# First layer of a four-layer convolution kernel: 8192-byte input runs, mirrored channels stored once, preparation over six groups, channel weights in ten pieces

## The chip, the cores and the metric

The kernel runs on one core of a Trainium2 chip. The time is the device time of one execution, in microseconds (us); given are the median of three executions and one more that was profiled. Engine names: PE is TensorE, PEld its weight loads, DVE VectorE, ACT ScalarE, POOL GpSimd, SP the queue of SyncE that issues DMAs.

## What is computed

The input `x` is float32 of shape (4, 16, 512, 512): four images of sixteen channels. Four layers follow each other, each `x + conv(gn(x))` or the like, `gn` a group norm over pairs of channels. The change is in the first only; layers 1 to 3 (a quantised 3x3 convolution, a 17-wide box filter, a convolution in Fourier space) read its result. The first layer is two denoise blocks, one behind the other:

```python
def _gn(v, G=8, eps=1e-5):
    ...
    return ((g - m) / jnp.sqrt(s + eps)).reshape(v.shape)
def _triplets(x):
    prev = jnp.where(idx == 0, 1, idx - 1)
    nxt = jnp.where(idx == T - 1, T - 2, idx + 1)
    return jnp.stack([x[:, prev], x, x[:, nxt]], axis=2)
def _denoise_block(x, w1, b1, w2, b2, w3, b3, a, b, c):
    ...
    o = a * _conv_reflect(xf, w1, b1, 1, 2) + b * _conv_reflect(xf, w2, b2, 2, 4) + c * _conv_reflect(xf, w3, b3, 4, 8)
    return jnp.tanh(o).reshape(B, T, H, W)
x = x + _L0_conv_ref(_gn(x), ...)
```

Each output channel is made of three neighbouring channels (at the ends of an image the missing neighbour is the mirrored one: channel 1 stands before channel 0, channel 14 behind channel 15) by 5x5 taps at dilations 1, 2 and 4 with reflected borders, and a tanh. The second block takes the first one's output; the residual is added behind it.

## The kernel before

`layer0` holds both blocks. A **unit** u is one half (256 rows) of one pair of channels of one image; there are 64 units a block, 16 an image, in the order image, pair p (0 to 7), half. A unit has four **groups** of 64 rows, so there are 512 groups; group n = 4u+g is 100 matmuls of 128x512 on PE (`products`, lines 688 to 728). In the trace block 0 runs from 79.93 us (its first matmul) to 1602.02, block 1 to 2989.65.

Between the passes the data lie in DRAM as float16 in two parts (a high and a low one, so that the pair carries nearly float32): `xs` holds the normalised input for block 0, `ys` block 0's output for block 1. Both have nine **pair-groups** an image: pair-group 0 holds channels 1 (mirrored) and 0, pair-group p channels 2p−1 and 2p, pair-group 8 channels 15 and 14 (mirrored). One row of one channel, high and low part with its reflected borders, is 2112 bytes.

A unit reads a **window** `win[half]` (named c_w in the trace): 128 partitions, two pair-groups interleaved by partition, 16 blocks of 16 rows with the rows above and below. For p = 0 both pair-groups must be loaded, for p ≥ 1 only pair-group p+1, since the other one is in the buffer already. `load(u, g)`, lines 903 to 925, loads a half-window (two groups) in three parts per pair-group, of 48, 8 and 8 partitions and 7 or 8 blocks, and at the image's border a fourth of 40 partitions; each row of a block is a run of 2112 bytes. It waits until PE has finished group 4(u−2)+g+1, six groups before the loaded rows are used (line 908).

The order of each engine's work is written out by hand, group by group:
- PE, `products(u, g)`: 60 matmuls straight from the window, then, where it is due, one of the two small matmuls `p0`, `p1_` of the preparation (lines 680 to 686, called at 710 to 714), 16 more from the window, 16 from `near` (c_n), 8 from `twice` (c). Behind group 14 and group 17 come two matmuls for the channel weights (lines 754 to 760).
- DVE, lines 656 to 676: copies for the next group (`near` and `twice`, L637 to L640), a preparation step, in group 15 `channel_weights` and in group 22 `scaled_weights`, then the low part of the output (`low`, L609) or, in block 1, the residual sum and extremes.
- ACT: one or two copies for the next group, the tanh out of PSUM, the high part.
- POOL: reflected borders; in block 1 tables for a later layer.
- SP, lines 979 to 1003: stores of prepared input, window loads, stores of the output (`store_y`, one DMA per channel and group, three for p = 0 and 7), in block 1 `store_x1`, `load_res` and `store_table`. `load_res(u)` waits at lines 930 and 931 for the use of the buffer and for the stores of x1 out of it.

**Preparation of an input pair i** (of 32) runs in four consecutive groups, one step a group: `v0` statistics of all rows (eight `bn_stats`, one `bn_aggr`), `v1` mean, `v2` reciprocal deviation and normalisation, `v3` the low part. `p0` and `p1_` sum over partitions on PE between `v0` and `v1`, and `v1` and `v2`, each in the group after the step. Pair i's first group is given by

```python
            return 64 * image + 4 + 7 * j + 2 * (i == 3) if i > 2 else -2
```

so seven groups lie between pairs. `load_x` (lines 888 to 894) reads a pair as eight DMAs of 256 KB, partitions of rows r, r+16, ...; `store_xs` writes its two channels to `xs`, and for the first and last pair of an image the mirrored channel a second time. The first three pairs are prepared before block 0 starts.

The change touches, besides, `first_group`, `steps` and `loads_x` (L359 to L365), `n_xs`, `stored`, `rows_in` (L380 to L395), which count what has been stored and loaded, and `views` (L412).

Of the kernel before, what the change touches and what calls it, by code (L numbers as in the profile page):

```python
# [9 lines left out]
ALU = mybir.AluOpType  # L10
# [271 lines left out]
def layer0(K):  # L282
# [9 lines left out]
    with ExitStack() as ctx:  # L292
# [47 lines left out]
        a_ld = [sem(f"a_ld{i}") for i in range(2)]  # L340
        a_sd, a_bn, a_p, a_rt, a_g, a_hi, a_lo, a_pad, w_sw = (sem("a_" + n) for n in ("sd", "bn", "p", "rt", "g", "hi", "lo", "pad", "sw"))
# [38 lines left out]
        def n_xs(i):  # L380

            return 16 * sum(2 + (r % 8 in (0, 7)) for r in range(i))
# [9 lines left out]
        def rows_in(e, u, g):  # L392

            n = sum(1 + (place(r)[2] == 0) for r in range(u % 2, u + 1, 2))
            e.wait_ge(c_ld[u % 2][g // 2], 16 * (3 + at_edge(u % 2, g)) * n)  # L395
# [16 lines left out]
        def views(i):  # L412

            xr = xin[i % 2][:, :, :].rearrange("p c (r w) -> p c r w", w=NW)
            if i == 1:
                return [(xr[:, c], yt[c][:, :, 0, PAD:PAD + NW], yt[c][:, :, 1, PAD:PAD + NW]) for c in range(2)]
            return [(xr, *(h[:, :, l, PAD:PAD + NW].rearrange("p (c r) w -> p c r w", c=2) for l in range(2)))]
# [14 lines left out]
        with nc.Block() as block:  # L432

            @block.vector
            def _(v):
                def v0(i):
                    v.wait_ge(a_ld[i % 2], 128 * (i // 2 + 1))
                    for j in range(8):
                        v.bn_stats(ast[:, j, :], xin[i % 2][:, j // 4, 512 * (j % 4):512 * (j % 4) + 512]).then_inc(a_bn, 1)
                    v.wait_ge(a_bn, 8 * (i + 1))  # L440
                    mark["m", i] = ch.step(v, v.bn_aggr(am[:, 0, :], ast[:, :, :].rearrange("p a b -> p (a b)")))
# [16 lines left out]
                def v3(i):  # L458
                    v.wait_ge(a_hi, i + 1)
                    for xr, hi, lo in views(i):  # L460
                        t = v.tensor_tensor(lo, xr, hi, ALU.subtract)
                    t.then_inc(a_lo, 1)
# [64 lines left out]
                def channel_weights():  # L527
                    v.wait_ge(w13_ld, 160)
                    v.wait_ge(w13_p, 1)
                    ch.step(v, v.tensor_copy(rp[:, :, :].rearrange("p j n -> p (j n)"), pq[:, 0:432]))  # L530
                    ch.step(v, v.memset(qf[:, :, :], 0.0))
                    rq = rp[:, 0, :].rearrange("p (o y x) -> p y x o", y=3, x=3)
                    for ro in range(8):
                        for ky in range(3):
                            ri = ro + ky - 1
                            if 0 <= ri < 8:
                                dst = qf[:, :, 16 * ro:16 * ro + 16]
                                ch.step(v, v.scalar_tensor_tensor(dst, rq[:, ky], pt[:, ri:ri + 1], dst, ALU.mult, ALU.add))
                    ch.step(v, v.tensor_copy(wq[:, 0], qf[:, :, :]))
                    ch.step(v, v.tensor_tensor(wq[:, 1], qf[:, :, :], wq[:, 0], ALU.subtract))  # L540
                    ch.step(v, v.memset(qf[:, :, :], 0.0))
                    for s_, to, ky in ((0, 0, 0), (1, 112, 2)):
                        q0, q2 = qf[:, 0, to:to + 16], qf[:, 1, to:to + 16]
                        ts(q0, rq[:, ky, 0], pt[:, 40 + s_:41 + s_])
                        ch.step(v, v.scalar_tensor_tensor(q0, rq[:, ky, 1], pt[:, 42 + s_:43 + s_], q0, ALU.mult, ALU.add))
                        ts(q2, rq[:, ky, 2], pt[:, 40 + s_:41 + s_])
                    ch.step(v, v.tensor_copy(K.whq[:, 0], qf[:, 0:2]))
                    ch.step(v, v.tensor_tensor(K.whq[:, 1], qf[:, 0:2], K.whq[:, 0], ALU.subtract))
                    ts(ur[:, 0], rr[:, 1], 1.0)
                    tt(ur[:, 1], rr[:, 0], rr[:, 2], ALU.add)  # L550
                    tt(ur[:, 2], rj[:, 0], rj[:, 2], ALU.subtract)
                    ts(ui[:, 0], rj[:, 1], 1.0)
                    tt(ui[:, 1], rj[:, 0], rj[:, 2], ALU.add)
                    tt(ui[:, 2], rr[:, 2], rr[:, 0], ALU.subtract)
                    for t in range(3):
                        six(ur[:, t], ui[:, t], [gm[:, t, 16 * f:16 * f + 16] for f in range(6)])
                    g3 = gm[:, 0:3, :].rearrange("p t n -> p (t n)")
                    tt(tfb[:, :], g3, g3, ALU.mult)
                    mark["g3"] = ch.step(v, v.tensor_reduce(c2b[:, 0:1], tfb[:, :], AX.X, ALU.add))

                def scaled_weights():
                    g3 = gm[:, 0:3, :].rearrange("p t n -> p (t n)")
                    v.wait_ge(w13_p, 2)
                    mark["sv"] = inverse(v, ch, w13_rt, 1, pq[:, 0:1], c2b, sv)
                    ts(g3, g3, sv[:, 0:1])
# [79 lines left out]
                v0(0), v1(0), v2(0)  # L645
                v0(1), v1(1)
                v3(0)
# [3 lines left out]
                v3(1)  # L651
                pieces()
                norms()
                v0(2), v1(2)
                copies(0)
                for u in range(2 * NU):
                    blk, b, p, half = place(u)
                    for g in range(4):
# [3 lines left out]
                        if i is not None:  # L662
                            (v0, v1, v2, v3)[s](i)
                        if (u, g) == (3, 2):
                            mark["v"] = ch.n
                        if (u, g) == (3, 3):
                            channel_weights()
                        if (u, g) == (5, 2):
                            scaled_weights()
# [9 lines left out]
            def _(p):  # L679
# [8 lines left out]
                def products(u, g):  # L688
# [17 lines left out]
                    rows4 = buf[:, 4 * g:4 * g + 4]  # L706
                    for di in (4, 0, 1, 7, 8):
# [41 lines left out]
                p1_(2)  # L749
                p.wait_ge(a_v, mark["wc"])  # L750
                for u in range(2 * NU):
                    for g in range(4):
                        products(u, g)
                        if (u, g) == (3, 2):
# [3 lines left out]
                        if (u, g) == (4, 1):  # L758
# [4 lines left out]
            def _(s):  # L763
                def hi(i):
                    s.wait_ge(a_g, i + 1)
                    if i > 1:
                        s.wait_ge(a_sd, n_xs(i))
# [1287 lines left out]
```

## Time and profile before

| what | value |
| --- | --- |
| time, median of 3 | 5130.97 us (5124.47 to 5133.29) |
| time of the profiled execution | 5131.47 us |
| its span in the trace | 5129.7 us |
| block 0, first matmul to block 1's first | 79.93 to 1602.02 us |
| block 1 | 1602.02 to 2989.65 us |
| PE busy, whole span | 4772.3 us (93%) |
| DVE, ACT, POOL busy | 4133.9 (81%), 4039.3 (79%), 1532.3 (30%) |
| DMA packets | 501930, 1161.93 MB, mean 227 GB/s |

The lines of a trace name the engine, the line of the kernel, the operation and the tiles (written <- read). A bracket tells how long the engine was idle before the instruction and what ended that. In a list of waits a line reads "engine, tile and line that waited <- what it waited for: us in total, times, longest". Tile names: c_w window, c_n `near`, c `twice`, c_p the PSUM of a group, a_x the input pair, a_st and a_mv its statistics, a_p the PSUM of the small matmuls, c_t and c_y output tiles, qf and rp weights.

### The profile page before, as it was taken

To read this page: it belongs to the slowest core of one execution; us is meant where nothing else is said; L and a number is where in the kernel's file an instruction comes from. 1 tells how busy PE (TensorE), PEld (TensorE's weight loads), DVE (VectorE), ACT (ScalarE), POOL (GpSimd) and SP (SyncE) were. 2 spreads that over 40 slices of the span, in tenths; PEclk is the share of its full clock that TensorE was granted. 3 is DMA by queue.
4 is the path that set the end of the run, shared out by engine and by line. 5 is a ranking of instruction groups with operands and counts; after the bars stand their busy time and mean duration, and the time that the engine had idled before them with its cause. 6 is when DMAs were issued, how large, how long until landed. Compare 5 with 4: busy or idle time off the path is not lost. (4 is left out here: it accounts for less than half of the span.)

```text
span 5129.7 us, 174298 instructions
## 1 busy us (share of the span) xinstructions
PE 4772.3 (93%) x74557; PEld 2805.2 (55%) x74557; DVE 4133.9 (81%) x7219; ACT 4039.3 (79%) x4023; POOL 1532.3 (30%) x1643
## 2 busy tenths in 40 slices
PE   4799999999999999999999979997776999999998
PEld 2344444445455795565566744434555566666665
DVE  5786786876867888888888868888999688888888
ACT  3576776776767888888888887876997799999897
POOL 0111111111113222222222100004776355555556
PEclk9899999999999999999999989998999999999999
DMA  8899899999978778788778769996886466666654
GB/s 220 224 246 261 249 266 255 248 259 252 247 211 236 221 217 240 230 221 248 220 229 243 216 235 324 323 325 236 308 309 247 114 150 153 150 153 150 153 150 119
DMA packets 501930, 1161.93 MB, mean 227 GB/s; under 512 B 59593, under 2 KB 60232, under 8 KB 468042
## 3 DMA queue, kind: packets, MB, share of 16 engines
q1 hardware_dynamic: 499000, 1148.40, 77.0%
q8 instruction: 592, 9.70, 0.8%
q10 hardware_dynamic: 2162, 2.39, 0.2%
q14 instruction: 176, 1.44, 0.1%
HBM read 678.71 MB, written 453.51 MB: 221 GB/s over the span
## 5 line engine op out<-in xcount | busy, mean ns | idle before, releaser
L702 PE MATMUL c_p<-c_w,wc 128*32 128x512 f16 x38912 | 2270.7, 380 | 53.5 <-DMA c_w<-xs 48.2
L702 PEld LDWEIGHTS c_p<-c_w,wc 128*32 128x32 f16 x38912 | 1239.7, 96 | 935.9 <-issue 42.7
L792 ACT ACTIVATE c<-c_w 64x2052 f16<-64x2052 f16 x512 | 984.7, 1923 | 87.3 <-DMA c_w<-xs 74.9
L778 ACT ACTIVATE c_t<-c_p,cbias,cscale 128x512 f32<-128x512 f32 x512 | 398.1, 777 | 541.2 <-PE c_p L702 538.6
L702 PE MATMUL c_p<-c_n,wc 128*32 128x512 f16 x8192 | 589.8, 381 | 20.4 <-DVE c_n L638 19.3
L1780 PE MATMUL f_P<-f_qh,f_wt 64*64 64x512 f16 x4608 | 545.7, 378 | 1.8 <-DVE f_t L1676 1.8
L1780 PE MATMUL f_P<-f_hl,f_wt 64*64 64x512 f16 x4608 | 545.3, 379 | 0.0
L884 POOL COPY c_y<-c_y 128x16 f16<-128x16 f16 x512 | 191.1, 401 | 1070.6 <-DVE c_y L609 1070.6
L794 ACT ACTIVATE c<-c_w 64x2052 f16<-64x2052 f16 x256 | 492.9, 1925 | 6.3
L1941 POOL TENSOR_TENSOR f_y<-f_y,f_x 128x512 f32<-128x512 f32 x256 | 330.8, 1292 | 449.4 <-DVE f_hl L1655 443.3
L1540 POOL TENSOR_TENSOR e_hl<-e_g,e_hl 128x2048 f16<-128x2048 f32 x63 | 257.2, 4083 | 608.4 <-ACT e_hl L1490 608.4
L637 DVE COPY c_n<-c_w 96x2112 f16<-96x2112 f16 x512 | 389.7, 761 | 58.7 <-DMA c_w<-xs 58.7
L1676 DVE SCALAR_TENSOR_TENSOR f_t<-f_P,f_kk,f_ci 128x256 f32<-128x256 f32 x1024 | 423.6, 476 | 13.5 <-PE f_P L1780 7.9
L609 DVE SCALAR_TENSOR_TENSOR c_y<-c_t,c_y 128x512 f16<-128x512 f32 x256 | 176.9, 691 | 272.8 <-ACT c_y L788 270.9
L1741 PE MATMUL f_qp<-f_hil,f_gT 128*128 128x260 f16 (+1 forms) x3120 | 392.0, 275 | 4.1 <-DVE f_qh L1660 4.1
L702 PEld LDWEIGHTS c_p<-c_n,wc 128*32 128x32 f16 x8192 | 276.4, 96 | 211.3 <-DVE c_n L637 20.2
L638 DVE COPY c_n<-c_w 32x2112 f16<-32x2112 f16 x512 | 368.5, 720 | 15.9
L1780 PEld LDWEIGHTS f_P<-f_hl,f_wt 64*64 64x64 f16 x4608 | 233.0, 106 | 255.0 <-issue 77.7
L702 PE MATMUL c_p<-c,wc 128*32 128x512 f16 x4096 | 366.7, 381 | 3.2 <-issue 3.2
L1169 PE MATMUL d_pp<-d_q,wq 128*128 128x512 f16 x1536 | 345.8, 381 | 17.4 <-DVE d_q L1066 17.4
L1915 ACT ACTIVATE f_y<-f_P,f_kk,sv 128x256 f32<-128x256 f32 x512 | 260.9, 560 | 128.0 <-PE f_P L1780 121.8
L1947 POOL TENSOR_TENSOR f_t<-f_t 128x512 f32<-128x512 f32 (+1 forms) x260 | 333.2, 1282 | 70.5 <-DVE f_hl L1655 70.5
(275 smaller groups left out, 7681.6 us busy)
## 6 DMA issues: line engine op xcount, KB each, us to landing
d_x<-x SPq DMA_DIRECT2D x128, 1024.0 KB, 7.8
x<-d_x SPq DMA_DIRECT2D x128, 1024.0 KB, 5.1
ys<-c_y SPq DMA_DIRECT2D x576, 132.0 KB, 6.7
xs<-a_hl SPq DMA_DIRECT2D x70, 1056.0 KB, 10.1
a_x<-in_x SPq DMA_DIRECT2D x256, 256.0 KB, 7.1
a_x<-in_x SPq DMA_DIRECT2D x128, 512.0 KB, 5.0
x<-a_x SPq DMA_DIRECT2D x512, 128.0 KB, 5.3
f_x<-x SPq DMA_DIRECT2D x256, 256.0 KB
```

The costliest lines, as they stand in the source:

```text
L637: v.tensor_copy(near[n % 2][0:96], w[0:96, :, 0:PW]).then_inc(c_nh, 1)
L638: v.tensor_copy(near[n % 2][96:128], w[64:96, :, PW:RW]).then_inc(c_nl, 1)
L702: t = p.matmul(pg[32 * j:32 * j + 32, :], weights[:, var], source[:, j, at:at + NW], start=start, stop=stop, tile_position=(0, 32 * j))
L778: s.activation(tt_[n % 3][:, :], pp[:, n % 4, :], ACT.Tanh, bias=cbias[:, blk:blk + 1], scale=cscale[:, blk:blk + 1]).then_inc(c_act, 1)
L792: s.activation(twice[n % 2][64:128, :, PAD - 2:PAD - 1 + NW], w[0:64, :, PW + PAD + 1:PW + PAD + 2 + NW], ACT.Copy).then_inc(c_2b, 1)
L794: s.activation(twice[n % 2][0:64, :, PAD - 2:PAD - 1 + NW], w[0:64, :, PW + PAD - 2:PW + PAD - 1 + NW], ACT.Copy).then_inc(c_2c, 1)
L1169: t = p.matmul(pp[:, 4 * (i % 2) + j, :], wq[:, wl, dx, :], qt[i % NQ][:, j, dx:dx + NW], start=(i < 2 and dx == 0 and wl == 0), stop=(i > ...
L1676: v.scalar_tensor_tensor(dst[0:n, z], src[:, 256 * z:256 * z + 256], k_[0:n, off + z:off + z + 1], cc_[0:n, j, z], op, ALU.mult).then_inc( ...
L1741: t = p.matmul(qp[0:n, a_, 0:260], T[:, xl, 1 - a_, kx, 0:n], hil[:, wl, 1 - a_, kx, :], start=z == 0, stop=z == 5)
L1780: t = p.matmul(P[64 * z:64 * z + 64, bank, :].rearrange("p (a i) -> p a i", a=2), w[k0:k0 + 64, wl, f, :], r[k0:k0 + 64, l, :, 0:256], sta ...
L1941: q.tensor_tensor(y0[i % 3][:, :, :], y0[i % 3][:, :, :], par(xin[i % NXF][:, :]), ALU.add).then_inc(f_ax, 1)
L1947: q.tensor_tensor(t1[i % 3][0:n], t1[i % 3][0:n], t2[i % 2][0:n], ALU.add).then_inc(f_aw, 1)
```

## The change

- Input rows lie four consecutive ones to a partition: a channel is one DMA of 1 MB in runs of 8192 bytes, a pair two DMAs instead of eight.
- The mirrored channels are not stored any more: two stores a pair into `xs`, two a group into `ys`. Instead the window of the first and last pair of an image takes the mirrored channel from where it is stored anyway: for p = 0 pair-group 0, for p = 7 pair-group 8 are loaded as two half sources of every second partition (24, 4 and 4 partitions in place of 48, 8 and 8; `sources`).
- The preparation takes six groups: `v0` per channel, `v1`, `v2`, `v3` per channel; high part, mirror and store go by channel as well. `p0` stands in the group of step 2 (after 60 matmuls), `p1_` in that of step 3 (after 24). Pairs start two groups earlier.
- `channel_weights` is cut into ten pieces at groups 15, 18, 22, 25, 29, 32, 36, 39, 43 and 46, `scaled_weights` into two at 50 and 57; PE's matmuls for them follow groups 14 and 48.
- The stores and loads at the start are put in another order, and the first two units' loads wait for the three stores that they need alone.

```diff
-            return 64 * image + 4 + 7 * j + 2 * (i == 3) if i > 2 else -2
-
-        steps = {first_group(i) + z: (i, z) for i in range(2, NG) for z in range(4) if first_group(i) + z >= 0}
-        loads_x = {first_group(i - 2) + 4 + 2 * c: (i, c) for i in range(4, NG) for c in range(2)}
+            return 64 * image + 2 + 7 * j + (i == 3) if i > 2 else -3
+
+        steps = {first_group(i) + z: (i, z) for i in range(2, NG) for z in range(6) if first_group(i) + z >= 0}
+        parts_at = [15 + 7 * (z // 2) + 3 * (z % 2) for z in range(10)]
+        loads_x = {first_group(i - 2) + 6 + 2 * c: (i, c) for i in range(4, NG) for c in range(2)}
...
-            e.wait_ge(c_yd[u % 2], 16 * sum(8 + 4 * (place(r)[2] in (0, 7)) for r in range(u % 2, u, 2)))
+            e.wait_ge(c_yd[u % 2], 128 * (u // 2))
+
+        def sources(p):
+
+            outer = {0: [(0, (0,), 1, 0), (0, (1,), 0, 1)], 7: [(8, (0,), 8, 0), (8, (1,), 7, 1)]}
+            return outer.get(p, []) + [(p + 1, (0, 1), p + 1, 0)] * (p < 7)
...
+                def v0(i, c):
+                    v.wait_ge(a_ld[i % 2], 32 * (i // 2 + 1))
+                    for j in range(4):
+                        v.bn_stats(ast[:, 4 * c + j, :], xin[i % 2][:, c, 512 * j:512 * j + 512]).then_inc(a_bn, 1)
+                    if c:
+                        v.wait_ge(a_bn, 8 * (i + 1))
+                        mark["m", i] = ch.step(v, v.bn_aggr(am[:, 0, :], ast[:, :, :].rearrange("p a b -> p (a b)")))
...
+                    if part < 4:
+                        for ro in (2 * part, 2 * part + 1):
+                            for ky in range(3):
+                                ri = ro + ky - 1
+                                if 0 <= ri < 8:
+                                    dst = qf[:, :, 16 * ro:16 * ro + 16]
+                                    ch.step(v, v.scalar_tensor_tensor(dst, rq[:, ky], pt[:, ri:ri + 1], dst, ALU.mult, ALU.add))
...
                     for di in (4, 0, 1, 7, 8):
+                        if s == 3 and di == 1:
+                            p1_(i)
                         for wl, xl in ((0, 0), (0, 1), (1, 0)):
...
-                    i, s = stage_of(n - 1)
-                    if s == 0:
+                    if s == 2:
                         p0(i)
-                    if s == 1:
-                        p1_(i)
...
-                        e.wait_ge(a_lo, i - 1)
-                    for c, r in ((c, r) for c in channels for r in range(4)):
-                        e.dma_start(xin[i % 2][:, c, NW * r:NW * r + NW],
-                                    dram(x, ((b * NC + 2 * g + c) * NH + 16 * r) * NW, [[NW, 16], [64 * NW, 8], [1, NW]])).then_inc(a_ld[i % 2], 16)
+                        e.wait_ge(a_lo, 2 * (i - 1))
+                    for c in channels:
+                        e.dma_start(xin[i % 2][:, c, :], dram(x, (b * NC + 2 * g + c) * NH * NW, [[4 * NW, 128], [1, 4 * NW]])).then_inc(a_ld[i % 2], 16)
...
-                    for gp in (0, 1) if p == 0 else (p + 1,):
+                    for gp, slots, of, slot in sources(p):
                         for to, count, row, j, banks in parts:
-                            e.dma_start(win[half][to + gp % 2:to + 2 * count:2, 4 * g + j:4 * g + j + banks],
-                                        dram(src, pair(b, gp, 256 * half + 64 * g + 16 * j + row), [[RW, count], [16 * YP, banks], [1, RW]])).then_inc(c_ld[half][g // 2], 16)
+                            at = dram(src, pair(b, of, 256 * half + 64 * g + 16 * j + row, slot), [[(3 - len(slots)) * RW, count * len(slots) // 2], [16 * YP, banks], [1, RW]])
+                            first_p = to + gp % 2 + 2 * slots[0]
+                            e.dma_start(win[half][first_p:to + 2 * count:6 - 2 * len(slots), 4 * g + j:4 * g + j + banks], at).then_inc(c_ld[half][g // 2], 16)
...
-                    for m, gp, slot in [(0, p, 1), (1, p + 1, 0)] + [(1, 0, 0)] * (p == 0) + [(0, 8, 1)] * (p == 7):
+                    for m, gp, slot in ((0, p, 1), (1, p + 1, 0)):
...
-                store_xs(0)
+                store_xs(0, 0)
+                store_xs(0, 1)
+                store_xs(1, 0)
                 load_x(2)
-                store_xs(1)
+                store_xs(1, 1)
```

## Rows read from the trace of the kernel before

**Rows 1.** By stretch: length, busy PE, PEld, DVE, ACT, POOL, PEclk, DMA share, GB/s.

```profile
79.93:1602.02 1522.09, 1435.36 (x25720) 738.44 (x25724) 1137.64 (x1809) 1047.86 (x890) 250.05 (x594) 0.98 0.91 246
1602.02:2989.65 1387.63, 1385.82 (x25604) 886.42 (x25596) 1163.50 (x2042) 1181.30 (x768) 285.71 (x362) 1.00 0.78 226
```

**Rows 2.** Waits of PE, whole span: total us, times, longest us.

```profile
PE a_p L682 <- DVE a_mv L441: 63.3, 28, 19.0
PE c_p L702 <- DMA c_w<-xs: 48.2, 10, 15.0
PE c_p L702 <- DVE c_n L638: 19.3, 2, 13.9
```

**Rows 3.** Waits of PE, from 0 to 85 us.

```profile
PE a_p L682 <- DVE a_mv L441: 39.1, 3, 19.0
```

**Rows 4.** Waits of PE in block 1, 1602 to 2990 us.

```profile
PE c_p L702 <- issue: 1.8, 5, 0.4
```

**Rows 5.** Timeline of PE, 390 to 410: start, length, instruction, count.

```profile
394.70 3.42 PE L702 MATMUL c_p<-c_w,wc 128*32 128x512 f16 x60
...
401.49 3.41 PE L702 MATMUL c_p<-c_w,wc 128*32 128x512 f16 x60
...
407.32 2.98 PE L702 MATMUL c_p<-c_w,wc 128*32 128x512 f16 x52
```

**Rows 6.** Timeline of DVE, 392 to 400.

```profile
393.71 4.83 DVE L439 BATCH_NORM_STATS2 a_st<-a_x 128x6 f32<-128x512 f32 x8
398.57 0.37 DVE L441 BATCH_NORM_AGGREGATE a_mv<-a_st 128x2 f32<-128x48 f32 x1
398.98 0.69 DVE L609 SCALAR_TENSOR_TENSOR c_y<-c_t,c_y 128x512 f16<-128x512 f32 x1
```

**Rows 7.** Timeline of DVE, 199 to 210: the channel weights' longest run.

```profile
200.32 7.39 DVE L538 SCALAR_TENSOR_TENSOR qf<-rp,pt,qf 128x48 f32<-128x48 f32 x22
```

**Rows 8.** Timeline of PE around the weights; in brackets the wait before.

```profile
201.30 1.04 PE L702 MATMUL c_p<-c_n,wc 128*32 128x512 f16 x16
...
220.74 1.90 PE L702 MATMUL c_p<-c_n,wc 128*32 128x512 f16 x16 [13.86 <-DVE c_n L638]
...
267.29 1.90 PE L702 MATMUL c_p<-c_n,wc 128*32 128x512 f16 x16 [5.43 <-DVE c_n L638]
...
269.81 5.10 PE L702 MATMUL c_p<-c_w,wc 128*32 128x512 f16 x76
```

**Rows 9.** Timeline of PE at the start: first, fourth and fifth half-window.

```profile
79.93 6.13 PE L702 MATMUL c_p<-c_w,wc 128*32 128x512 f16 x76 [12.94 <-DMA c_w<-xs]
...
118.53 5.62 PE L702 MATMUL c_p<-c_w,wc 128*32 128x512 f16 x76 [3.07 <-DMA c_w<-xs]
...
147.70 5.52 PE L702 MATMUL c_p<-c_w,wc 128*32 128x512 f16 x60 [15.03 <-DMA c_w<-xs]
```

**Rows 10.** By stretch: first window loads, one image edge of block 1.

```profile
64.40:118.50 54.10, 35.95 (x604) 19.14 (x604) 24.83 (x38) 23.46 (x19) 3.93 (x12) 0.99 0.94 198
1917.00:1990.00 73.00, 72.29 (x1334) 43.90 (x1330) 59.15 (x103) 61.60 (x41) 12.76 (x17) 1.00 0.87 244
```

**Rows 11.** PE timeline, image edges of block 0: first and last of six.

```profile
505.08 4.29 PE L702 MATMUL c_p<-c_w,wc 128*32 128x512 f16 x76 [3.48 <-DMA c_w<-xs]
...
1266.84 5.97 PE L702 MATMUL c_p<-c_w,wc 128*32 128x512 f16 x76 [3.94 <-DMA c_w<-xs]
```

**Rows 12.** Timeline of SP at an image edge of block 1, 1910 to 1990.

```profile
1916.90 5.78 SPq L924 DMA_DIRECT2D c_w<-ys  x8
...
1927.39 7.17 SPq L924 DMA_DIRECT2D c_w<-ys  x6
...
1976.68 2.90 SPq L924 DMA_DIRECT2D c_w<-ys  x4
```

**Rows 13.** Waits of SP, 1917 to 1990.

```profile
SPq L931 <- DMA x<-a_x: 16.4, 2, 8.6
```

**Rows 14.** DMA issues: out<-in, queue, count, KB each, median us to landing.

```profile
f_es<-f_es SPq DMA_DIRECT2D x4, 32.0 KB, 1.8
```

More of the change, by code:

```diff
@@ L340, in layer0 @@
         a_ld = [sem(f"a_ld{i}") for i in range(2)]
+        a_s1 = [sem(f"a_s1{i}") for i in range(2)]
         a_sd, a_bn, a_p, a_rt, a_g, a_hi, a_lo, a_pad, w_sw = (sem("a_" + n) for n in ("sd", "bn", "p", "rt", "g", "hi", "lo", "pad", "sw"))
@@ L378, in pair, with inputs_stored @@
             return ((b * 9 + g) * NH + row) * YP + slot * RW
-        def n_xs(i):
-            return 16 * sum(2 + (r % 8 in (0, 7)) for r in range(i))
+        def inputs_stored(e, i):
+            e.wait_ge(a_sd, 32 * (i - (i > 1)))
+            if i > 1:
+                e.wait_ge(a_s1[0], 16)
+                e.wait_ge(a_s1[1], 16)
         def stored(e, u):
-            e.wait_ge(c_yd[u % 2], 16 * sum(8 + 4 * (place(r)[2] in (0, 7)) for r in range(u % 2, u, 2)))
+            e.wait_ge(c_yd[u % 2], 128 * (u // 2))
+        def sources(p):
+            outer = {0: [(0, (0,), 1, 0), (0, (1,), 0, 1)], 7: [(8, (0,), 8, 0), (8, (1,), 7, 1)]}
+            return outer.get(p, []) + [(p + 1, (0, 1), p + 1, 0)] * (p < 7)
         def at_edge(half, g):
@@ L392, in rows_in @@
         def rows_in(e, u, g):
-            n = sum(1 + (place(r)[2] == 0) for r in range(u % 2, u + 1, 2))
+            n = sum(len(sources(place(r)[2])) for r in range(u % 2, u + 1, 2))
             e.wait_ge(c_ld[u % 2][g // 2], 16 * (3 + at_edge(u % 2, g)) * n)
@@ L414, in views @@
             xr = xin[i % 2][:, :, :].rearrange("p c (r w) -> p c r w", w=NW)
-            if i == 1:
-                return [(xr[:, c], yt[c][:, :, 0, PAD:PAD + NW], yt[c][:, :, 1, PAD:PAD + NW]) for c in range(2)]
-            return [(xr, *(h[:, :, l, PAD:PAD + NW].rearrange("p (c r) w -> p c r w", c=2) for l in range(2)))]
+            return [(xr[:, c], t[:, :, 0, PAD:PAD + NW], t[:, :, 1, PAD:PAD + NW]) for c, t in enumerate(halves_of(i))]
         def halves_of(i):
@@ L435, in _ @@
             def _(v):
[L436 to L441, printed above, removed]
+                def v0(i, c):
[5 more added lines that the diff above has]
+                        mark["m", i] = ch.step(v, v.bn_aggr(am[:, 0, :], ast[:, :, :].rearrange("p a b -> p (a b)")))
                 def v1(i):
@@ L456, in v2, with v3 @@
                     v.wait_ge(a_g, i + 1)
[L458 to L462, printed above, removed]
+                def v3(i, c):
+                    v.wait_ge(a_hi, 2 * i + c + 1)
+                    xr, hi, lo = views(i)[c]
+                    v.tensor_tensor(lo, xr, hi, ALU.subtract).then_inc(a_lo, 1)
                 def taps():
@@ L566, in scaled_weights @@
+                def scaled_weights(part):
+                    if part == 0:
+                        g3 = gm[:, 0:3, :].rearrange("p t n -> p (t n)")
+                        v.wait_ge(w13_p, 2)
+                        mark["sv"] = inverse(v, ch, w13_rt, 1, pq[:, 0:1], c2b, sv)
+                        ts(g3, g3, sv[:, 0:1])
+                        return
                     q = slice(0, 48)
@@ L763, in _, with hi @@
             def _(s):
[L764 to L767, printed above, removed]
-                    for xr, hi_, lo_ in views(i):
-                        t = s.activation(hi_, xr, ACT.Copy)
-                    t.then_inc(a_hi, 1)
+                def hi(i, c):
+                    if c == 0:
+                        s.wait_ge(a_g, i + 1)
+                        if i > 1:
+                            s.wait_ge(a_sd, 32 * (i - 1))
+                    s.activation(views(i)[c][1], views(i)[c][0], ACT.Copy).then_inc(a_hi, 1)
                 def evict(u, g):
@@ L865, in _ @@
                 q.memset(win[0][:, 0, :], 0.0).then_inc(c_z, 1)
-                mirror(0)
-                mirror(1)
+                mirror(0, 0), mirror(0, 1)
+                mirror(1, 0), mirror(1, 1)
                 q.wait_ge(w_hi, 6)
@@ L875, in _ @@
                         i, s = stage_of(4 * u + g)
-                        if s == 3:
-                            mirror(i)
+                        if s in (4, 5):
+                            mirror(i, s - 4)
                         if table_of(u) is not None and g % 2 == 0:
```

148 lines of the change are left out of this document (74 added, 74 removed).

## The prediction

> **What bounds the kernel now.** I read the profile from coarse to fine. First the stretches of the span, cut at the first matmul of each pass: the reader should see that the first pass (block 0) lasts 1522.1 us with TensorE (PE) busy 1435.4, the second (block 1) 1387.6 with PE busy 1385.8, so block 1 has 1.8 us to give and block 0 has 86.7 [rows 1]. Block 1's 256 groups are 5.42 us each; that is PE's pace. Layers 1 to 3 are not touched by the diff and are left out.
>
> Next, what PE waited for in the whole span [rows 2], less what it waited before block 0 begins [rows 3, 9]: group-norm sums 63.3−39.1 = 24.2 us in 25 waits; window loads 48.2−12.9 = 35.3 in 9; the near copies on VectorE (DVE) 19.3 in 2. Together 78.8 of the 86.7. In block 1 PE waited only for its own issue [rows 4]. The DMA engines are busy 0.91 of block 0 and 0.78 of block 1 [rows 1].
>
> The measure is the profiled execution, 5131.5 us (span 5129.7 and 1.8 around it); the median of three is 5131.0, so the two can be used alike. About 0.2%, 10.3 us, can be told from no change: faster is below 5121, slower above 5142.
>
> **Part 1: preparation over six groups.** A group with `p0` in it takes 401.49−394.70 = 6.79 us, the one with `p1_` 407.32−401.49 = 5.83, an ordinary one 5.42 [rows 5]. Of the first, 24.2/25 = 0.97 us is waiting; the rest, 0.4 us each, is the small matmuls themselves and stays. Why PE waits: DVE begins the eight statistics 4.43 us into a group and needs 4.83+0.37 us [rows 6], so they end 4.2 us into the next group, while PE asks after 60 matmuls, 3.42 us into it. After the change a group does four statistics. The second half and the aggregate end 4.43+2.4+0.4 = 7.2 us after their group's start; PE asks at 5.42+3.42 = 8.8. `p1_`, after 24 matmuls of the following group, asks 6.7 us after the start of the group in which DVE's `v1` runs; `v1` starts at 4.43 and is three one-column operations, under 1.1 us by the 0.37 of an aggregate. Both are early, by 1.6 and 1.2 us. Behind DVE's own waits for the two sums stand the low part and the next copies, but the sums are there 0.6 and 2.7 us before DVE comes to them (3.8 and 1.7 us into a group against 4.43). On SP, counted in groups, the input loads stay where they were (4+4 = 2+6), now two issues in place of eight; they come 6 groups, 32.5 us, before the statistics that wait for both, and `v3` of the older pair that they wait for is over a group earlier. The first channel's store moves one group ahead, past one window load, with one issue where there were two or three together. Splitting activation, subtraction, mirror and store by channel makes more, smaller instructions on ScalarE, DVE and GpSimd, hidden under PE (DVE is busy 75% of block 0, ScalarE 69%, GpSimd 16% [rows 1]); without that cover it would be some 0.4 us for each of four extra instructions. Price of the waits: −24.2 at best, 0 if a new wait of the same size takes their place; I take −24.2, the end that the margins point to.
>
> **Part 2: channel weights in ten pieces.** Two waits for the near copies, 13.86 and 5.43 us [rows 8]: the copies queue on DVE behind the weights, of which 22 operations alone take 7.39 us [rows 7], 0.34 each. In six of them at most, with two small ones before them, a piece is about 3 us. A group without a preparation step uses three copies and a low part, 4×0.7 = 2.8 us of DVE [rows 6], so 2.6 us are free, and the copies run one group ahead, which takes up a remainder. The last piece (35 operations, under 12 us at 0.34 each, and they are narrower) has 2.6 us free in each of its own group and the next ones and may leave 0 to 4 us; I take 0, as it stands in a group of no step. The two PE matmuls for the weights move to where their operands are a group old. Gain 19.3. TensorE also runs slower just after such waits: 16 matmuls take 1.90 against 1.04, 76 take 5.10 [rows 8] against 4.29 [rows 11]; with eight more at the same ratio that is 2×(0.86+0.43)+0.81 = 3.4 us. Part 2: −22.7; with 4 us left by the last piece and 2.1 of slow matmuls behind them, −16.6.
>
> **Part 3: 8192-byte input runs, mirrored channels not stored.** Two input DMAs in place of eight a pair, two stores instead of three at an image's ends: less traffic and fewer issues on SyncE (SP). This is worth only what waits for DMAs: in block 0 35.3 us in nine waits, of which 15.0 and 3.1 (and a third wait, of 0.8) at the start and 16.4 in six at image edges [rows 9, 11]. It is paid for in part 4.
>
> **Part 4: windows of pairs 0 and 7 from narrower DMAs.** This decides. The first four half-windows (all of pair 0) start 79.93 to 118.53, 12.87 us apart [rows 9], with the DMA engines 0.94 busy at 198 GB/s [rows 10]. Per engine that is 198/16/0.94 = 13.2 GB/s, 0.160 us for a 2112-byte run. 
>
> The Trainium skill, page "DMA: Bandwidth & Descriptors", section "Why a DMA increments its semaphore by 16 and not by 1", states that such a DMA uses the largest number of engines up to 16 that divides the slowest dimension of both sides, the lowest-numbered ones. 
> What the edge costs in block 1: between 1917 and 1990 share 0.87 at 244 GB/s [rows 10] is 0.120 us a run. Beside a half-window's loads two groups bring 36 more runs per engine (stores of x1 16, residual 16, table 4). Pair 0 before: 116×0.120 = 13.9 us against 10.84 in which PE uses one up. Four in a row take 55.7, the last is due at 32.5 and needed six groups later, at 65.0. It fits, and PE waits for nothing [rows 4]. SP shows the lag: loads due every 10.84 us from 1916.90; the fifth is due at 1960.3 and issued at 1976.68 [rows 12], 16.4 late, of which 4×13.9−43.4 = 12.4 is this arithmetic and 4.0 SP standing at line 931 for the x1 stores, 16.4 us in two waits [rows 13].
> After: pair 7's four take (64+36)×0.120 = 12.0 each, pair 0's four (104+36)×0.120 = 16.8, 115.2 in all; with SP's 4.0 and a landing of at least 1.8 [rows 14], 121.0. The last is needed at 7×10.84+32.5 = 108.4: 12.6 late, in two waits of about six microseconds. Three edges inside block 1: 37.8. Each wait brings slow matmuls behind it, 2.1 us by those behind the 5.43 [rows 8]: six of them, 12.6. Block 0's edges see the same narrow loads but lighter stores and a shorter queue: 0, between −16 (their waits go) and +31 (24×8×0.160 uncovered at one of the three). The start: 0, between −10 (earlier stores) and +15 (4×24 runs×0.160).
>
> **Sum.** 5131.5−24.2−22.7+37.8+12.6 = 5135.0. Block 0 some 45 us shorter, block 1 some 50 longer.
>
> **Rivals.** B, the narrow loads don't bind: their runs spread over engines well enough, or the six groups of lead hide them. For it: block 1's DMA share is 0.78 overall [rows 1], and the 80 rests on one division. Against: 12.87 us instead of the 10.2 that 64 runs give. Then 5131.5−46.9, and with block 0's 16.4 of edge waits and 10 of the start gone, about 5058.
> C, slower: the edge's run costs more than 0.120 us. The kernel before, where no wait was seen, allows up to (65.0−1.8)/(4×116) = 0.136 with SP's hold counted in it. Then the eight half-windows take 4×100×0.136+4×140×0.136 = 130.6, the last is 130.6+1.8−108.4 = 24.0 late, three edges 72: 34 more than forecast, 5169. From 0.123 us a run on the kernel is measurably slower. For it: the start's 0.160. Against: that stretch had loads and stores of other shapes in it.
> D, the sums are late in their new places too (a wait on `p1_` replaces that on `p0`): +24.2, 5159. Against: the margins of 1.2 and 1.6 us worked out above.
>
> **Chances.** Forecast 0.55, its own range 5117 to 5154 (half or one and a half times the edge waits): faster 0.07, same 0.31, slower 0.17. B 0.20, all faster. C 0.20 and D 0.05, slower. Faster 0.27, same 0.31, slower 0.42. The range is 5080 to 5172: it takes in C at its worked-out price, D, and B where block 0's edges still wait; the rest of B, some 0.15, and a still dearer C, 0.05, are left out.
>
> **What would show it.** Right: PE waiting for window loads from ys about 12 us at each of three edges of block 1, 1.8 us of issue elsewhere; no wait for the sums after the start; none for the near copies; block 0 near 1475, block 1 near 1438; SP further behind at line 931's counterpart. Wrong: block 1 still at 1388 (B), edges at 24 us each (C), 25 waits for sums (D), or block 0's edge waits doubled.

## The result: faster by 0.73%, and where the time went

The changed kernel takes 5091.39 us (median of four, 5086.73 to 5094.86) against 5128.26 of the kernel before in the same comparison: a ratio of 0.9927, 95% interval 0.9910 to 0.9944. Forecast were 5135.0 us and no change that can be told from none; the time lies in the range of 5080 to 5172, but on its faster side. The profiled execution took 5093.15 us, its span is 5091.2.

The span by stretch, block 0 and block 1, with the columns of [rows 1]:

```profile
74.46:1540.62 1466.16, 1422.02 (x25722) 739.35 (x25726) 1140.69 (x1839) 1047.55 (x920) 267.71 (x654) 0.99 0.84 244
1540.62:2944.26 1403.64, 1390.37 (x25604) 978.67 (x25596) 1161.47 (x2042) 1181.05 (x768) 288.40 (x362) 1.00 0.75 223
```

The start is 5.5 us shorter (79.93 to 74.46), block 0 55.9 shorter (forecast 47), block 1 16.0 longer (forecast 50). What lies behind block 1, where nothing was changed, is 2146.9 us long against 2140.1; over the fourteen profiles of this study it varies between 2137 and 2148, so this part of the difference is put down to no cause.

The waits of PE in the whole span, which answer to [rows 2]:

```profile
PE a_p L704 <- DVE a_mv L450: 65.7, 12, 19.2
...
PE c_p L724 <- DVE c_n L655: 16.2, 7, 5.0
PE c_p L724 <- DMA c_w<-xs: 16.2, 5, 11.8
```

Before block 0 they are 36.7 us in 3 times and, for the first window, 11.8:

```profile
PE a_p L704 <- DVE a_mv L450: 36.7, 3, 15.1
PE c_p L724 <- DMA c_w<-xs: 11.8, 1, 11.8
```

So inside the blocks the group-norm waits are 29.0 us in 9 times, but 22 of these are two waits at the start (19.16 at 126 us, 2.89 at 166), where PE waited 18.9 us for windows before [rows 9]:

```profile
126.43 0.58 PE L704 MATMUL a_p<-a_mv,ones 128*128 128x1 f32 x2 [19.16 <-DVE a_mv L450]
```

The other seven are 7.0 us together, six of them at image edges; before there were 25 waits. Window loads cost 4.4 against 35.3, the near copies in block 0 2.9 against 19.3. New is what PE waits for in block 1, where it waited for nothing before [rows 4]:

```profile
PE c_p L724 <- DVE c_n L655: 13.3, 3, 5.0
```

Three waits, at 1926.73, 2279.40 and 2631.93, one in the second pair-0 unit of each image but the first. That is where the forecast had put them, but not for the reason it gave: they wait for DVE's near copies, not for a window load. DVE, PE and SP around the first of them:

```profile
1922.64 0.69 DVE L634 TENSOR_TENSOR a_x<-c_t,a_x 128x512 f32<-128x512 f32 x1 [8.38 <-DMA a_x<-in_x]
...
1925.16 0.70 DVE L654 COPY c_n<-c_w 96x2112 f16<-96x2112 f16 x1
1925.88 0.70 DVE L655 COPY c_n<-c_w 32x2112 f16<-32x2112 f16 x1
```

```profile
1918.96 4.34 PE L724 MATMUL c_p<-c_w,wc 128*32 128x512 f16 x76
1926.73 1.52 PE L724 MATMUL c_p<-c_n,wc 128*32 128x512 f16 x16 [3.43 <-DVE c_n L655]
```

```profile
1884.56 1.41 SPq L955 DMA_DIRECT2D a_x<-in_x  x2
1886.08 6.41 SPq L945 DMA_DIRECT2D c_w<-ys  x9
...
1895.72 9.99 SPq L945 DMA_DIRECT2D c_w<-ys  x12
...
1916.60 1.41 SPq L955 DMA_DIRECT2D a_x<-in_x  x2
```

PE starts the 76 window matmuls at 1918.96 without a wait: the window is there. DVE's last work before that sum ended at 1914.26; from then on it stands for the **residual** of the unit (a_x), whose DMA goes out at 1916.60, two microseconds after DVE wants it. Behind DVE's sum stand the near copies of the group after, and behind those PE.

SP issues the residual late because it stands at line 951, as at line 931 before, for the stores of x1 out of the same buffer. In block 1 as changed this stand is

```profile
SPq L951 <- DMA x<-a_x: 158.8, 52, 9.3
```

It is not new, and DVE's wait for the residual is not either. The kernel before has, with 12.7 us in three waits of DVE at the same places of the three images:

```profile
SPq L931 <- DMA x<-a_x: 160.6, 53, 9.2
1975.16 1.41 SPq L935 DMA_DIRECT2D a_x<-in_x  x2
1982.30 0.69 DVE L617 TENSOR_TENSOR a_x<-c_t,a_x 128x512 f32<-128x512 f32 x1 [4.58 <-DMA a_x<-in_x]
```

There PE did not notice. With the narrow loads SP has 21 window DMAs to issue for this unit instead of 14, and counted from the start of block 1 the residual goes out 2.8 us later (1916.60−1540.62 = 375.98 against 1975.16−1602.02 = 373.14). DVE's three waits grow to 8.38, 9.74 and 9.51 us; PE's are 3.43, 4.85 and 4.99, so a lead of 4.5 to 5.0 us is used up first.

### The profile page after: what moved, and what is told of

It reads as the page before. It is cut to its first block and busy times, and to the rows that moved or that the text cites. A ratio compares the mean times of both kernels' runs of the same rounds, so it can differ in the third digit from the quotient of the medians.

```text
span 5091.2 us, 174514 instructions
## 1 busy us (share of the span) xinstructions
PE 4768.7 (94%) x74557; PEld 2899.5 (57%) x74557; DVE 4134.3 (81%) x7250; ACT 4039.1 (79%) x4054; POOL 1557.4 (31%) x1705
## 5 line engine op out<-in xcount | busy, mean ns | idle before, releaser
L724 PE MATMUL c_p<-c_w,wc 128*32 128x512 f16 x38912 | 2229.6, 379 | 17.9 <-DMA c_w<-xs 16.2
L724 PEld LDWEIGHTS c_p<-c_w,wc 128*32 128x32 f16 x38912 | 1295.0, 96 | 820.0 <-issue 24.8
L724 PE MATMUL c_p<-c_n,wc 128*32 128x512 f16 x8192 | 557.3, 381 | 16.8 <-DVE c_n L655 16.2
L1698 DVE SCALAR_TENSOR_TENSOR f_t<-f_P,f_kk,f_ci 128x256 f32<-128x256 f32 x1024 | 423.5, 475 | 12.7 <-PE f_P L1802 8.0
L634 DVE TENSOR_TENSOR a_x<-c_t,a_x 128x512 f32<-128x512 f32 x256 | 193.0, 754 | 207.9 <-ACT c_t L798 178.2
## 6 DMA issues: line engine op xcount, KB each, us to landing
a_x<-in_x SPq DMA_DIRECT2D x64, 1024.0 KB, 11.8
```

Source lines behind the costliest of these rows:

```text
L724: t = p.matmul(pg[32 * j:32 * j + 32, :], weights[:, var], source[:, j, at:at + NW], start=start, stop=stop, tile_position=(0, 32 * j))
L1698: v.scalar_tensor_tensor(dst[0:n, z], src[:, 256 * z:256 * z + 256], k_[0:n, off + z:off + z + 1], cc_[0:n, j, z], op, ALU.mult).then_inc( ...
```

## The experiments

All runs are of whole kernels; each median is set against the kernel before in the same session (5121 to 5126 us).

**Windows whole in block 1 only, ys's mirrored channels stored again.**

```diff
+            if u >= NU:
+                return [(0, (0, 1), 0, 0)] * (p == 0) + [(p + 1, (0, 1), p + 1, 0)]
...
-                    for m, gp, slot in ((0, p, 1), (1, p + 1, 0)):
+                    for m, gp, slot in [(0, p, 1), (1, p + 1, 0)] + [(1, 0, 0)] * (p == 0) + [(0, 8, 1)] * (p == 7):
```

> The changed kernel, with the mirrored channels of ys stored again and block 1's windows loaded whole as before; block 0 reads xs by the half sources. Theory (the half sources of pairs 0 and 7 cost block 1 its extra 16 us): block 1 back from 1403 to 1388 us and PE's three waits for the near copies (13.3 us at groups 326, 390 and 454) gone; block 0 has 64 more stores of 135 KB at its image edges and loses 0 to 16 us of that; 5075 to 5091 in all. Rival (what delays block 1's loads is SP standing behind the stores of x1, whatever shape the loads have): block 1 stays at 1400 or more, 5091 to 5107.

5078.0 us, ratio 0.9906 (0.9892 to 0.9920). Block 1 lasts 1388.2 us, its waits for near copies are one of 1.9; block 0 is 7.8 longer than as changed. As the theory said: the shape of the loads is behind block 1's 16 us.

```profile
74.11:1548.11 1474.00, 1426.13 (x25722) 753.66 (x25726) 1140.42 (x1839) 1047.74 (x920) 266.22 (x654) 0.99 0.86 249
1548.11:2936.31 1388.20, 1385.05 (x25604) 799.56 (x25596) 1164.52 (x2042) 1181.09 (x767) 287.26 (x362) 1.00 0.78 225
```

**Windows whole in both blocks.** The same in xs: `store_xs` writes the mirrored channel again, `sources` knows no half sources.

> The changed kernel, with the mirrored channels stored again in both xs and ys and all windows loaded whole as before; preparation, weights and 8192-byte runs stay as changed. Theory: block 1 at 1388 (16 less); block 0 gets the edge waits of the kernel before back, 16.4 us against 3.8 now, so 12 more there; about 5087. Rival (the stores left out gave a good part of block 0's gain, the narrow loads cost it nothing): block 0 30 us longer or more, 5105 or above.

5052.5 us, ratio 0.9856 (0.9843 to 0.9869): faster than both kernels, by 73 us of before and 36 to 39 of the changed one (by the ratios and by the medians). Both expectations were wrong, and the gain is larger than either allowed. Its stretches and PE's waits in block 0:

```profile
73.68:1526.79 1453.11, 1424.10 (x25722) 751.07 (x25726) 1141.00 (x1839) 1047.56 (x920) 267.06 (x654) 0.99 0.89 257
1526.79:2911.58 1384.79, 1384.50 (x25606) 922.39 (x25596) 1165.83 (x2042) 1181.44 (x768) 286.41 (x362) 1.00 0.78 226
```

```profile
PE a_p L708 <- DVE a_mv L454: 19.1, 6, 12.7
PE c_p L728 <- DMA c_w<-xs: 10.3, 1, 10.3
PE c_p L728 <- issue: 8.2, 11, 1.7
PE c_p L728 <- DVE c_n L659: 1.6, 1, 1.6
```

The first wait of 10.3 stands ahead of block 0; the edges of block 0 have no wait for a window left. So the edge waits before, 16.4 us, were not the price of storing mirrored channels. In block 0 the half sources of xs cost 20.9 us (1474.0 against 1453.1, both with ys stored twice), although they save stores; against the changed kernel, which saves the stores of ys as well, block 0 is 13.1 shorter.

**Residual loads one group later.**

```diff
-                        if g == 0 and NU + 2 <= u + 1 < 2 * NU:
+                        if g == 1 and NU + 2 <= u + 1 < 2 * NU:
```

> The changed kernel with the residual loads of block 1 issued one group later, behind that group's window loads, so that SP stands for the stores of x1 with no window load due behind it for a group. Theory (SP's stand, 158.8 us in 52 waits, puts the late loads later): the loads of the second half of pair 0 go out 4 to 8 us earlier, PE's three waits of 13.3 us are gone or under 3, block 1 about 1388, 5076 in all. Rival (the DMA engines set the pace at the edge and the stand only shows it): the waits stay at 10 or more, 5091.

5100.3 us, ratio 0.9950 (0.9936 to 0.9963), block 1 1416.4. A miss on both sides, and the run that gave the cause away: at the first edge SP no longer stood at the line. The nine window loads of the second unit's first half went out at 1879.03 instead of 1886.08, the residual behind them at 1891.54 instead of 1884.56, and PE's waits in block 1 nearly doubled.

```profile
PE c_p L724 <- DVE c_n L655: 24.6, 3, 9.3
```

```profile
1905.53 0.69 DVE L634 TENSOR_TENSOR a_x<-c_t,a_x 128x512 f32<-128x512 f32 x1 [11.80 <-DMA a_x<-in_x]
```

DVE stood 11.80 us for that residual. The theory that the window loads are late fell here, and that of the late residual took its place.

**Four residual buffers, one unit ahead.**

```diff
-            return xin[u % 2][:, 0, :].rearrange("p (g w) -> p g w", w=NW)
+            return xin[u % 2][:, u // 2 % 2, :].rearrange("p (g w) -> p g w", w=NW)
...
-                    if r >= 2:
-                        e.wait_ge(c_mm, 8 * (r - 1))
-                        e.wait_ge(c_1d[u % 2], 128 * (r // 2))
+                    if r >= 4:
+                        e.wait_ge(c_mm, 8 * (r - 3))
+                        e.wait_ge(c_1d[u % 4], 128 * (r // 4))
```

> The changed kernel (narrow windows, nothing stored twice) with four residual buffers in block 1 in place of two: the second channel halves of the two input tiles, unused in block 1, take part, so a residual load waits for the stores of x1 four units back, not two. Theory (PE's three waits in block 1 are residuals that land late: the load stands behind stores of x1, which stand behind the narrow window loads; DVE's sum waits for it and the next near copies behind the sum): the waits of 13.3 us are gone, SP's stand of 158.8 us too, block 1 1388 to 1392 us, 5077 in all. Rival (the window loads themselves are too late, as the forecast had it): the waits stay at 10 us or more, 5091.

5088.6 us, ratio 0.9935 (0.9922 to 0.9948), block 1 1398.8. SP's stand is gone, the waits are not (10.4 us). The residual goes out at 1909.87, seven us before DVE asks for it, but behind the twelve window loads, and DVE has it only 16.4 us later, at 1926.30; the median load of this kind lands after 5.3. The window issued ahead of it comes late too: ACT's copy waits for it until 1921.42.

```profile
1921.42 1.92 ACT L812 ACTIVATE c<-c_w 64x2052 f16<-64x2052 f16 x1 [4.48 <-DMA c_w<-ys]
1926.30 0.69 DVE L634 TENSOR_TENSOR a_x<-c_t,a_x 128x512 f32<-128x512 f32 x1 [9.71 <-DMA a_x<-in_x]
```

```profile
1897.10 9.39 SPq L945 DMA_DIRECT2D c_w<-ys  x12
1906.53 3.23 SPq L968 DMA_DIRECT2D x<-a_x  x4
1909.87 2.57 SPq L955 DMA_DIRECT2D a_x<-in_x  x2
```

**Four residual buffers, two units ahead.** As above, with `load_res(u + 2)` in place of `load_res(u + 1)` and a semaphore per buffer.

> The changed kernel with four residual buffers in block 1 (as in narrow_res_four) and the residual loads issued two units ahead instead of one. In narrow_res_four DVE still stood 9.7 us for a residual that SP, late behind the narrow loads, had issued 7 us before its use. Theory (block 1 loses its time through late residuals): the waits for the near copies at groups 326, 390 and 454 (13.3 us as changed, 10.5 with one unit ahead) fall under 2, block 1 lasts 1393 us or less against 1403, about 5080 in all. Rival (with the residuals gone the window loads themselves are late): 10 us of waiting stay under another name, 5088 or more.

5070.0 us, ratio 0.9894 (0.9879 to 0.9909). Block 1 is at PE's pace with every narrow window load still in it, and PE's only wait there is for its own issue:

```profile
1543.04:2927.82 1384.78, 1384.36 (x25607) 913.68 (x25596) 1163.08 (x2042) 1180.25 (x768) 289.48 (x362) 1.00 0.78 226
```

```profile
PE c_p L724 <- issue: 0.3, 1, 0.3
```

That settles block 1: with the residual early enough the narrow windows are in time, so the whole 16 us came through the residual. What makes it late is SP's stand and issues in the changed kernel, and in the run before this one, as the late window there suggests, the transfers ahead of it.

**The weights alone**, in the kernel before: ten pieces in groups 15, 17, 22, ... 45, the scaled weights in groups 51 and 52.

> The kernel before with nothing but the channel weights in ten pieces (in groups 15 to 45, two of each seven that have no preparation step) and the scaled weights in two. Theory: the two waits of 19.3 us and 3.4 us of slow matmuls are gone, 5105 against 5128. Rival (block 0 is held by its DMAs, so time won early comes back as waiting at the next image edge): less than 10 us, 5118 or above.

5109.9 us, ratio 0.9969 (0.9956 to 0.9981): 15.9 us, between the two expectations. Both waits for near copies are gone. My placement brought a new wait of 8.09: the last piece in group 52 stood on DVE ahead of the statistics of group 53, and PE waited for these.

```profile
425.40 0.58 PE L692 MATMUL a_p<-a_mv,ones 128*128 128x1 f32 x2 [8.09 <-DVE a_mv L442]
```

Without it the pieces would be worth 24.0, an estimate (15.9 and the 8.1 of that wait) near the forecast's 22.7. In the profiles block 0 is 24.7 us shorter even with that wait (1497.4 against 1522.1), so this part is known only to within several us. The changed kernel puts that piece into group 57 and has a wait of 1.96 behind it.

**The statistics in one group again**, otherwise the kernel with whole windows.

```diff
-                            if s < 2:
-                                v0(i, s)
+                            if s == 1:
+                                v0(i, 0), v0(i, 1)
+                            elif s == 0:
+                                pass
```

> The same kernel of 5052.5 us, with all eight statistics of a pair in one group again (step 1; step 0 does nothing), and the two small matmuls where the change puts them. Theory (the group-norm waits went because the statistics are spread over two groups): PE waits about 0.9 us in each of 25 or more groups for them, 20 to 25 us more, 5073 to 5078. Rival (block 0 is held by its DMAs, so such waits are caught up at the next edge): 10 us or less, 5062 at most.

5076.6 us, ratio 0.9908 (0.9893 to 0.9923): 24.1 us more by the medians, 26.7 by the ratios (the two kernels ran in different sessions). From 180 us to the end of block 0 PE waits 27 times for them, 28.4 us, against 1.9 in 4 times with two groups:

```profile
PE a_p L710 <- DVE a_mv L454: 28.4, 27, 2.7
```

The theory held, and the waits were not caught up at an edge.

**2048-byte input runs again**, otherwise the kernel with whole windows (rows r, r+16, ... to a partition, eight DMAs a pair).

> The kernel of the run with both tensors stored twice (5052.5 us), with the input read again in runs of 2048 bytes, eight DMAs a pair, rows r, r+16, ... to a partition. Theory (the 8192-byte runs free the DMA engines, and the three image edges of block 0 use it): 10 to 27 us come back there, 5063 to 5079. Rival (the edges' gain comes from the order of stores and preparation, not from the runs): under 5 us, 5057 at most.

5078.2 us, ratio 0.9921 (0.9906 to 0.9936): 25.7 us more by the medians, 33 by the ratios. Block 0 is 19.6 longer, the start 5.1.

```profile
78.82:1551.52 1472.70, 1423.97 (x25722) 733.71 (x25726) 1140.30 (x1839) 1047.55 (x920) 265.49 (x654) 0.99 0.93 254
```

The DMA engines move fewer bytes a second (254 against 257) with a larger share of their time (0.93 against 0.89). The packet records of the two traces show two sources of that: in block 0 four runs of 2048 bytes take 4×0.1324 = 0.530 us and one of 8192 takes 0.471, and the 2112-byte runs beside them take 0.120 us against 0.115. The edit also turns 64 DMAs of 1 MB into 256 of 256 KB and stores xs in another row order; no run separates these from the length of the runs.

**8192-byte runs alone**, in the kernel before (the stores to xs follow the new row order):

```diff
-                    for c, r in ((c, r) for c in channels for r in range(4)):
-                        e.dma_start(xin[i % 2][:, c, NW * r:NW * r + NW],
-                                    dram(x, ((b * NC + 2 * g + c) * NH + 16 * r) * NW, [[NW, 16], [64 * NW, 8], [1, NW]])).then_inc(a_ld[i % 2], 16)
+                    for c in channels:
+                        e.dma_start(xin[i % 2][:, c, :], dram(x, (b * NC + 2 * g + c) * NH * NW, [[4 * NW, 128], [1, 4 * NW]])).then_inc(a_ld[i % 2], 16)
```

> The kernel before with nothing but the input rows in runs of 8192 bytes (two DMAs a pair, four consecutive rows to a partition, the stores to xs laid out to match). Theory (the runs free DMA time that block 0's image edges and the start wait for): 20 to 28 us less than before, 5094 to 5102. Rival (they help only once the statistics no longer make PE wait): 10 us less at most, 5112 or more.

5103.1 us, ratio 0.9953 (0.9940 to 0.9966): 22.7 us less. From 80 to 1600 us PE waits for window loads 11.0 us in two waits, one of 10.9, where there were nine of 35.3 (first window left out). Of the 16.4 us at image edges 0.16 are left, with whole windows and every mirrored channel stored: those waits were the price of the input's DMAs. The first group begins at 71.54 instead of 79.93. Some of the gain went into waits for PE's own issue (18.8 us against 7.6).

```profile
PE a_p L682 <- DVE a_mv L441: 26.0, 26, 2.6
PE c_p L702 <- issue: 18.8, 21, 2.5
...
PE c_p L702 <- DMA c_w<-xs: 11.0, 2, 10.9
```

```profile
133.89 5.10 PE L702 MATMUL c_p<-c_w,wc 128*32 128x512 f16 x60 [10.89 <-DMA c_w<-xs]
507.86 4.29 PE L702 MATMUL c_p<-c_w,wc 128*32 128x512 f16 x76 [0.16 <-DMA c_w<-xs]
```

**Three runs on ends and start.** Only pair 7 narrow (its channel 14 not stored twice), pair 0 whole:

> The kernel of 5052.5 us with pair 7's windows from the half sources (channel 14 not stored a second time in xs and ys), pair 0's whole. Theory (pair 0 is what overruns: 104+36 runs on the busiest engine against 80+36; pair 7's 64+36 fit into the 10.84 us of a step, as its loads landed in 9.4 us): no loss, 5045 to 5056. Rival (every narrow load costs in proportion to its extra runs, half of the 39 us at each end): 5068 to 5076.

5065.2 us, ratio 0.9887 (0.9870 to 0.9905), between the two: inconclusive. It is 12.7 us above the kernel with all windows whole by the medians, 8.5 in the profiled executions; of these blocks 0 and 1 have 4.2, and 4.7 lie behind block 1, where the kernels are alike.

Input of pair 3 ahead of unit 1's windows, in the kernel with whole windows (`load_x(3)` behind unit 0's loads):

> The same kernel of 5052.5 us, with the input load of pair 3 issued before unit 1's window loads instead of behind them. Theory (PE's wait of 12.7 us at 118.9 is for statistics whose input was queued behind 42 narrow or 28 whole window loads): that wait falls by about 8 us, 5040 to 5047. Rival (unit 1's windows come as much later and PE waits for those): the same or a few us slower, 5052 to 5058.

5056.4 us, ratio 0.9870 (0.9856 to 0.9883): the rival. The wait for statistics at 118.9 us is gone, others came for the windows and for pair 4's statistics.

```profile
105.32 1.05 PE L728 MATMUL c_p<-c_w,wc 128*32 128x512 f16 x8 [7.38 <-DMA c_w<-xs]
```

```profile
162.52 0.59 PE L708 MATMUL a_p<-a_mv,ones 128*128 128x1 f32 x2 [9.73 <-DVE a_mv L454]
```

The same input between unit 1's two loads, with only pair 7 narrow:

> The kernel of narrow_p7_only with the input load of pair 3 between the two window loads of unit 1. Theory (three windows first, then the input: no window is needed sooner than it lands, and the statistics come 4 us earlier): 3 to 6 us less than narrow_p7_only. Rival (the start is bound by the sum of its DMAs in whatever order, as whole_x3_early showed): within 3 us of it.

5062.3 us, ratio 0.9874 (0.9859 to 0.9889), 2.9 us below narrow_p7_only: just within what its rival allowed, and too close to the theory's 3 to decide. In both runs with another order PE waits less for statistics and more for windows; that the start is bound by the sum of its DMAs in whatever order fits this but is not shown.

## Why the prediction was wrong

**Part 1, the statistics: right.** Forecast −24.2; taking them back costs 24.1 to 26.7. The 25 waits are gone but for seven (7.0 us), and the `p1_` margin held. The forecast did not see the 22 us of statistics waits at the start; they took the place of window waits there.

**Part 2, the weights: right, as far as measured.** Forecast −22.7; alone −15.9, and an estimated −24.0 without the wait that my own placement of the last piece added.

**Part 3, the input runs: the step that failed.** The forecast set it at 0: "This is worth only what waits for DMAs: in block 0 35.3 us in nine waits" and then "It is paid for in part 4". The row with the 35.3 us was the price, and it was not used: alone the new input loads bring 22.7, with 16.2 of the 16.4 us of edge waits gone; taken back they cost 25.7 to 33. I had priced the traffic saved only where it met the narrow loads, and let two terms cancel that do not: the narrow loads cost at the edges of both blocks, the input loads help at the start and at the edges of block 0.

The Trainium skill, page "DMA: Bandwidth & Descriptors", section "Specifications", gives 512 bytes as the least transfer for line rate. By that the runs of 2048 bytes had nothing to gain from being longer. In block 0 of these traces 8192 bytes take 0.471 us as one run and 0.530 as four, and the measurement decides; how much of the 22.7 us is the length of the runs, and how much the fewer and larger DMAs, no run here shows.

**Part 4, narrow windows: right in sign, wrong in place, size and mechanism.** Forecast +50.4, all of it in block 1, and 0 in block 0 and the start. Measured by undoing it: 36 to 39 in all, of which block 1 has 18.9 (1403.64 against 1384.79) and block 0 13.1 (1466.16 against 1453.11). Three steps of it:
- "12.6 late, in two waits" did not come. The window of the last pair-0 half was there when ACT copied from it, 3.0 us before PE began on it at 1918.96:

```profile
1915.99 1.92 ACT L812 ACTIVATE c<-c_w 64x2052 f16<-64x2052 f16 x1 [1.38 <-DMA c_w<-ys]
```

  Shares and rates by stretch, four half-windows of pair 7, then four of pair 0:

```profile
1811.00:1855.00 44.00, 44.00 (x822) 38.72 (x816) 36.77 (x65) 37.61 (x25) 9.73 (x12) 1.00 0.67 216
1855.00:1917.00 62.00, 62.00 (x1153) 50.65 (x1148) 50.25 (x91) 52.09 (x35) 13.17 (x16) 1.00 0.74 223
```

  By the forecast's own formula a run costs 2112×16×0.67/216 = 105 ns for pair 7 and 112 for pair 0, not 120. Pair 7's 100 runs are 10.5 us and fit into 10.84, so no backlog of 4.6 is handed to pair 0, and pair 0's four are 4×140×0.008 = 4.5 shorter. That is 9 of the 15.6 us between 12.6 late and 3.0 early; the other 6.5 stay open. (The forecast's 12.4 for 4×13.9−43.4 is 12.2 by its own terms, without effect.)
- What was late was the residual. The forecast counted the residual among the 36 other runs and SP's stand at line 931 as a delay of window loads, but never asked who waits for what SP issues there, though DVE already waited for it before. Rival C goes with this step: by the same formula the price of a run fell instead of rising.
- Block 0: "0, between −16 and +31" held in its bounds, not in its value: 13.1 net, made up of 20.9 for the half sources of xs and 7.8 saved by the stores of ys left out.

Sum with measured terms: −24.1−24.0−22.7 and +36 to +39 make −32 to −35; with the larger values of parts 1 and 3, by the ratios, it is down to −48. Measured are −36.9, so the terms add up only roughly. The forecast was 43.6 us too high: 22.7 of this is part 3, 11 to 14 are part 4, 3.2 come from starting at 5131.5 where the comparison has 5128.3, and the rest is within the scatter. With part 3 at its measured value the forecast's own sum would have been 5112 and faster.

**Rivals.** B gave 5058 for narrow loads that cost nothing; without them the kernel stands at 5052.5, so its sum was about right, partly by luck, and its condition was not met: the 26.4 us of edge waits and start that it took for cheap narrow loads are what the input loads brought. D did not happen.

## What to carry to other kernels

When a wait on a resource stands in the rows, whatever relieves the resource is worth up to that wait: give it a term of its own, and do not let it cancel against a cost elsewhere. When a queue is slowed, list everything that is issued behind it on that queue and ask of each transfer who waits for it; the one that comes late need not be one that was changed. A change of several parts that measures little should be taken apart: here three parts were worth 73 us together (5052.5 against 5125.8) and the fourth took half of that back. And look at waits that are covered today: the residual's 12.7 us cost nothing before and decided block 1 afterwards.

## What was not expected of the hardware

By the forecast's formula, a mean over all packets by their bytes, a run cost 0.120 us at a share of 0.87 [rows 10] and 0.112 and 0.105 at the changed edge. The packet records give it directly: a 2112-byte packet took 0.134 us at the edge before, 0.134 between edges of the changed kernel (1640 to 1800 us, share 0.76), and 0.122 and 0.117 where its pairs 0 and 7 are loaded (shares 0.74 and 0.67). So a count of runs on the busiest engine times the price of another stretch overstated the time here. That the uneven load is the reason is not shown: in block 0 with whole windows the same packets take 0.115 at a share of 0.89, and no record says on which engine a packet ran.

With input DMAs of 2048-byte runs in place of 8192 the same bytes took block 0 from a share of 0.89 to 0.93 and 19.6 us longer. PE's waits for its own issue changed from profile to profile, 2.2 us in block 0 as changed and 18.8 with only the longer runs; no run here shows why.
